# The routed experts of a gated block: order of gather and addition on GpSimd, row numbers cast on VectorE, gated rows turned inside the up products

## The reference

```python
xn = _rmsnorm(x, w_ln2)
shared = mean(_experts(xf, sWg, sWu, sWd))          # one shared expert, all rows
probs = softmax(xf @ Wgate + expert_bias)           # 8 experts
topk_p, topk_i = top_k(probs, 2)                    # two experts a row, shares scaled to sum 1
# _experts: silu(x @ Wg) * (x @ Wu) @ Wd, with 512 -> 256 -> 512
routed = einsum('ne,nec->nc', comb, _experts(xf, Wg, Wu, Wd))
x + tanh(g_ffn) * (residual + shared + routed)
```

## Time and profile before

| what | value |
|---|---|
| timed runs | 2496.61, 2498.39, 2503.72 us; median 2498.39 |
| the profiled execution's own time | 2492.11 us |
| its span, first to last instruction | 2490.3 us |
| TensorE busy | 2193.2 us (88% of the span) |
| VectorE, ScalarE, GpSimd busy | 61%, 48%, 56% |
| TensorE's granted clock, mean | 0.959 of full speed |

### The profile page before, as it was taken

One profiled execution on the slowest core, in us unless ns is written; L12 is line 12 of the kernel. 1 busy time (PEld: TensorE's weight loads), 2 busy tenths in 40 slices (PEclk: granted clock), 3 DMA queues, 4 the chain that ended last, 5 costly groups with the idle time before them and its releaser, 6 DMA issues. The chain is left out here.

```text
span 2490.3 us, 50414 instructions
## 1 busy us (share of the span) xinstructions
PE 2193.2 (88%) x12864; PEld 977.9 (39%) x12865; DVE 1506.9 (61%) x4072; ACT 1201.2 (48%) x2316; POOL 1401.2 (56%) x1598
## 2 busy tenths in 40 slices
PE   3699999999999963899999999999948887898887
PEld 1233333333333211444444444444424443444443
DVE  4588888887888733656655566565526783333332
ACT  3255555555555433354544545455445653444443
POOL 3177767677676751365654655546534664555554
PEclk9899999999999986999999999999978898999999
DMA  4413223232232204452533524334234764555554
GB/s 155 151 48 111 90 87 109 72 107 96 86 116 71 71 26 130 140 147 86 151 118 111 147 90 146 116 118 130 80 107 86 165 148 91 97 93 93 94 92 79
DMA packets 221402, 264.60 MB, mean 106 GB/s; under 512 B 37400, under 2 KB 163468, under 8 KB 220852
## 3 DMA queue, kind: packets, MB, share of 16 engines
q1 hardware_dynamic: 197628, 212.81, 28.2%
q0 software_dynamic: 22976, 48.38, 11.3%
q10 hardware_dynamic: 520, 0.27, 0.0%
HBM read 162.12 MB, written 86.80 MB: 100 GB/s over the span
## 5 line engine op out<-in xcount | busy, mean ns | idle before, releaser
L464 ACT ACTIVATE a_pt<-a_bank 128x512 f32<-128x512 f32 x512 | 305.1, 597 | 361.2 <-DVE a_bank L567 349.2
L1345 DVE CUSTOM_DVE_ANT_0 b_bank<-b_bank,b_tri 128x256 f32<-128x256 f32 (+3 forms) x512 | 253.7, 498 | 322.2 <-PE b_bank L1483 319.8
L578 DVE CUSTOM_DVE_ANT_0 a_bank<-a_bank,a_strip 128x512 f32<-128x512 f32 x512 | 354.8, 693 | 21.5 <-PE a_bank L721 18.8
L1130 POOL TENSOR_TENSOR b_acc<-b_acc,b_pt 128x256 f32<-128x256 f32 (+2 forms) x384 | 271.7, 725 | 105.6 <-ACT b_pt L1219 88.9
L374 POOL TENSOR_TENSOR a_acc<-a_acc,a_pt 128x512 f32<-128x512 f32 x256 | 317.6, 1271 | 12.8 <-ACT a_pt L464 9.3
L567 DVE TENSOR_TENSOR a_bank<-a_bank,a_band 128x256 f32<-128x256 f32 (+1 forms) x512 | 205.9, 403 | 132.3 <-PE a_bank L708 130.5
L1219 ACT ACTIVATE b_pt<-b_bank 128x256 f32<-128x256 f32 (+2 forms) x384 | 143.3, 381 | 203.5 <-PE b_bank L1467 199.5
L721 PE MATMUL a_bank<-a_k_stack,a_q_stack 97*128 97x512 f16 x512 | 197.7, 387 | 17.5 <-DMA a_k_stack<-mask_rows 10.7
L708 PE MATMUL a_bank<-a_q_stack,a_k_stack 128*128 128x512 f16 x512 | 197.6, 387 | 15.4 <-ACT a_pt L464 11.4
L1812 POOL DMA_INDIRECT out_dram<-c_z,c_to_row x72 | 115.1, 1598 | 144.1 <-DMA out_dram<-c_z,c_to_row 117.0
L2203 DVE SCALAR_TENSOR_TENSOR c_hid<-c_th,c_bank 128x256 f32<-128x256 f32 x72 | 30.3, 421 | 229.6 <-ACT c_th L1954 228.2
(11 more groups left out here) (337 smaller groups left out, 5632.7 us busy)
## 6 DMA issues: line engine op xcount, KB each, us to landing
b_q_stack<-qk_rows SPq DMA_DIRECT2D x192, 128.0 KB, 2.7
a_q_stack<-qk_rows SPq DMA_DIRECT2D x96, 128.0 KB
a_k_stack<-qk_rows SPq DMA_DIRECT2D x96, 128.0 KB
b_k_stack<-qk_rows SPq DMA_DIRECT2D x96, 128.0 KB, 2.6
a_xn<-in_x SPq DMA_DIRECT2D x32, 256.0 KB, 2.6
a_cn<-in_ctx SPq DMA_DIRECT2D x32, 256.0 KB, 3.1
qk_rows<-a_qk_hi SPq DMA_DIRECT2D x64, 128.0 KB, 1.7
qk_rows<-a_qk_lo SPq DMA_DIRECT2D x64, 128.0 KB, 1.8
```

The source lines that it names most:

```text
L464: nc.scalar.activation(pt[:, n % SLOTS, :], st_bank[n % 2][:], ACT.Exp).then_inc(exped, 1)
L578: nc.vector.tensor_tensor_reduce(out=max_bank[step % 2][:], in0=max_bank[step % 2][:], in1=strip[:, g * HG + hh, at:at + S], scale=-1.0, s ...
L1130: nc.gpsimd.tensor_tensor(sums_of, sums_of, probs(n), ALU.add).then_inc(pooled, 1)
L1345: nc.vector.tensor_tensor_reduce(out=max_bank[step % 2][:, 0:w], in0=max_bank[step % 2][:, 0:w], in1=tri[:, at:at + w], scale=-1.0, scalar ...
```

## The change

On GpSimd the gather of block j+3 stands ahead of the addition of block j-2, the casts of both kinds of row numbers are gone, and the register for the landing is loaded ahead of the waits. VectorE casts the row numbers: four `from_row` ahead of the loop, then that of block j+4 behind the low part of block j+1, and `to_row` of block j at the end of step j, which from the fourth block on waits for the addition four blocks before (the buffer's last reader). ScalarE scales the gathered rows of block j+2 ahead of the high hidden part of block j-1, and its output waits for `to_set`. On TensorE the gated rows are turned behind the first three of the twelve up products, and each register is loaded where its products begin. In the last batch of the dense part all eight `scatter` DMAs follow one another, the low part is on VectorE, `lay_starts` stands behind the first `activate`, and `add_to_output` of that batch stands behind the first three gathers.

```diff
--- before.py
+++ after.py
@@ -1766,6 +1766,9 @@
                 if b:
                     add_to_output(b - 1)
                 write_records(b)
+                if b + 1 == B:
+                    scatter(b, range(NT))
+                    continue
                 if b > 1:
                     scatter(b, (0,))
                 low_part(b, 0)
@@ -1782,22 +1785,19 @@
                     rms(b + 2)
                 if b == 1:
                     scatter(1, range(NT))
-            add_to_output(B - 1)
 
             def gather(at):
                 j, u = at.n, at.slot
-                pool.wait_ge(entered[u], at.use * 16 + 32)
+                pool.wait_ge(from_set, j + 1)
                 if not at.within(0, 3):
                     pool.wait_ge(x_turned, j + (AHEAD - 3))
                 pool.nop(nofuse=True)
-                nc.gpsimd.tensor_copy(from_row[:, u, :], entry[:, bass.ds(j, 1), 0]).then_inc(from_set, 1)
-                pool.wait_ge(from_set, j + 1)
-                pool.nop(nofuse=True)
                 pool.indirect_dma_start(x_in[:, u], None, z_all, bass.IndirectOffsetOnAxis(from_row[:, u, :], 0)).then_inc(gathered[u], 16)
 
             def scatter_add(at):
                 j, u = at.n, at.slot
-                nc.gpsimd.tensor_copy(to_row[:, u, :], entry[:, bass.ds(j, 1), 1]).then_inc(to_set, 1)
+                if not at.within(0, 0):
+                    landed_before = pool.value_load(block_i[0:1, 2, bass.ds(j, 1)], min_val=16, max_val=8 * NB)
                 pool.wait_ge(to_set, j + 1)
                 pool.nop(nofuse=True)
                 pool.wait_ge(y_ready, j + (AHEAD + 1))
@@ -1806,7 +1806,6 @@
                     pool.wait_ge(added[u % 2], at.use * 32 + u // 2 * 16)
                     pool.nop(nofuse=True)
                 if not at.within(0, 0):
-                    landed_before = pool.value_load(block_i[0:1, 2, bass.ds(j, 1)], min_val=16, max_val=8 * NB)
                     pool.wait_ge(added[(u + 1) % 2], landed_before)
                     pool.nop(nofuse=True)
                 pool.indirect_dma_start(out_rows, bass.IndirectOffsetOnAxis(to_row[:, u, :], 0), y_out[:, u], None, compute_op=ALU.add
@@ -1815,16 +1814,15 @@
             pool.wait_ge(out_stored[2], 32)
             for j in range(3):
                 gather(Count(0, j, 4))
+            add_to_output(B - 1)
             for i in range(3):
                 pool.wait_ge(out_stored[i], 16 * ((B - i + 2) // 3))
 
             def step(at):
+                if not at.within(NB - 3, NB):
+                    gather(at.back(-3))
                 if not at.within(0, 1):
                     scatter_add(at.back(2))
-                if at.within(NB - 3, NB):
-                    pool.sem_inc(from_set, 1)
-                else:
-                    gather(at.back(-3))
             over(pool, step)
             scatter_add(Count(0, NB - 1, 4))
 
@@ -1942,19 +1940,19 @@
                     x_high(0, 0)
                 if not at.within(NB - 1, NB):
                     x_high(j + 1, u + 1)
+                if not at.within(NB - 2, NB):
+                    scale_rows(at.back(-2))
                 if not at.within(0, 0):
                     act.wait_ge(x_hid_turned, j + AHEAD)
                     act.wait_ge(x_down, j + (AHEAD - 2))
                     nc.scalar.activation(hidden_rows(h_hi, u + 1), hid_bank[(u + 1) % 2][:, 0:I], ACT.Copy).then_inc(x_h_hi, 1)
-                if not at.within(NB - 2, NB):
-                    scale_rows(at.back(-2))
                 if not at.within(NB, NB):
                     act.wait_ge(x_up, j + (AHEAD + 1))
                     act.wait_ge(x_half, j + (AHEAD - 1))
                     nc.scalar.activation(hidden_rows(th, u), up_bank[u % 2][:, 0:I], ACT.Tanh, scale=0.5 / WS).then_inc(x_tanhed, 1)
                 if not at.within(0, 0):
                     act.wait_ge(x_down, j + AHEAD)
-                    act.wait_ge(from_set, j + 3)
+                    act.wait_ge(to_set, j)
                     nc.scalar.activation(y_out[:, last.slot], down_bank[(u + 1) % 2][:], ACT.Copy, scale=entry[:, bass.ds(last.n, 1), 2]
                                          ).then_inc(y_ready, 1)
             over(act, step)
@@ -2130,6 +2128,10 @@
                 v.scalar_tensor_tensor(out=hid[:, i, :], in0=hid[:, i, :], scalar=DOWN, in1=chunk_bank[2 * i + 1][:], op0=ALU.mult,
                                        op1=ALU.mult).then_inc(hidden, 1)
 
+            def low_part(i):
+                dve.wait_ge(h_hi_done, NI * (B - 1) + i + 1)
+                v.tensor_tensor(h_lo[:, i, :], hid[:, i, :], h_hi[:, i, :], ALU.subtract).then_inc(h_lo_done, 1)
+
             def finish_rows(b, t):
                 dve.wait_ge(downed, NT * b + t + 1)
                 dve.wait_ge(gated, NT * b + t + 1)
@@ -2158,15 +2160,18 @@
                 place_rows(b)
                 if b == 0:
                     find_spare()
+                activate(b, 0)
                 if not more:
                     lay_starts()
-                activate(b, 0)
+                    low_part(0)
                 if more:
                     low(b + 1, 0)
                     low(b + 1, 1)
                 if b:
                     up_weights(b)
                 activate(b, 1)
+                if not more:
+                    low_part(1)
                 if more:
                     low(b + 1, 2)
                     low(b + 1, 3)
@@ -2186,12 +2191,26 @@
                 v.tensor_tensor(xt_lo[:, u % 2, :, 0:P], turn_bank[u % 2][:].rearrange("p (k q) -> p k q", q=P), xt_hi[:, u % 2, :, 0:P],
                                 ALU.subtract).then_inc(x_lo_done, 1)
 
+            def set_from_row(at):
+                dve.wait_ge(entered[at.slot], at.use * 16 + 32)
+                v.tensor_copy(from_row[:, at.slot, :], entry[:, bass.ds(at.n, 1), 0]).then_inc(from_set, 1)
+
+            def set_to_row(at):
+                if not at.within(0, 3):
+                    dve.wait_ge(added[at.slot % 2], at.use * 32 + (at.slot // 2 * 16 - 16))
+                v.tensor_copy(to_row[:, at.slot, :], entry[:, bass.ds(at.n, 1), 1]).then_inc(to_set, 1)
+
+            for j in range(4):
+                set_from_row(Count(0, j, 4))
+
             def step(at):
                 j, u = at.n, at.slot
                 if at.within(0, 0):
                     x_low(0, 0)
                 if not at.within(NB - 1, NB):
                     x_low(j + 1, u + 1)
+                if not at.within(NB - 4, NB):
+                    set_from_row(at.back(-4))
                 if not at.within(0, 0):
                     w = (u + 1) % 2
                     dve.wait_ge(x_h_hi, j + AHEAD)
@@ -2205,6 +2224,7 @@
                     dve.wait_ge(x_half, j + (AHEAD + 1))
                     v.scalar_tensor_tensor(out=hidden_rows(hid, w), in0=hidden_rows(hid, w), scalar=DOWN, in1=up_bank[w][:, I:2 * I],
                                            op0=ALU.mult, op1=ALU.mult).then_inc(x_hidden, 1)
+                    set_to_row(at)
             over(dve, step)
 
         @block.tensor
@@ -2309,8 +2329,8 @@
                     last = nc.tensor.transpose(turn_bank[u % 2][:, k * P:(k + 1) * P], rows[:, k * P:(k + 1) * P], idn[:])
                 last.then_inc(x_turned, 1)
 
-            def x_up_to(j, u, e):
-                w = u % 2
+            def x_up_to(at, e):
+                j, u, w = at.n, at.slot, at.slot % 2
                 pe.wait_ge(x_lo_done, j + (AHEAD + 1))
                 pe.wait_ge(x_hidden, j + (AHEAD - 1))
                 for k in range(NK):
@@ -2319,6 +2339,8 @@
                     mm(up_bank[w][:], xt_hi[:, w, k, 0:P], weights(gu_hi), start=(k == 0), stop=False)
                     mm(up_bank[w][:], xt_hi[:, w, k, 0:P], weights(gu_lo), start=False, stop=False)
                     last = mm(up_bank[w][:], xt_lo[:, w, k, 0:P], weights(gu_hi), start=False, stop=(k == NK - 1))
+                    if k == 0 and not at.within(0, 0):
+                        turn_hidden(at.back(1).n, u + 1)
                 last.then_inc(x_up, 1)
 
             def turn_hidden(j, u):
@@ -2351,22 +2373,19 @@
 
             def step(at):
                 j, u = at.n, at.slot
-                own = earlier_x = None
                 if not at.within(NB, NB):
                     own = expert_of(at)
-                if not at.within(0, 0):
-                    earlier_x = expert_of(at.back(1))
                 if at.within(0, 0):
                     x_turn(x_in[:, 0], 0, 0)
                 if not at.within(NB - 1, NB):
                     after = at.back(-1)
                     x_turn(x_in[:, after.slot], after.n, after.slot)
+                if at.within(NB, NB):
+                    turn_hidden(at.back(1).n, u + 1)
+                else:
+                    x_up_to(at, own)
                 if not at.within(0, 0):
-                    turn_hidden(at.back(1).n, u + 1)
-                if not at.within(NB, NB):
-                    x_up_to(j, u, own)
```

(3 more changed lines are left out.)

## The result

The changed kernel takes 2433.9 us (median of 4, 2432.3 to 2436.6) against 2497.5 for the kernel before on the same chip: ratio 0.9743 (95%: 0.9725 to 0.976). The forecast was 2435, with a range of 2424 to 2470. The profiled execution took 2433.8 us (span 2432.0), 58.3 under that of before.

The account below looks back on a forecast made before the run. GpSimd's own list of work was taken as the bound; 69 steps from 5.58 to 4.65 us gain 64.2, end costs 1, hand-over 0: -63 us, median 2498.4 to 2435, range 2424 to 2470.

Parts of the forecast that it names:

- The bound: Routed part: GpSimd's own list of work sets the 5.58 us per block; the landing falls beside it by chance.
- GpSimd's new turn: GpSimd's steady rhythm: between 3.20 us (lower bound, 0.30 between indirect DMAs) and 5.16 us (upper), no longer the bound.
- Rival (1): GpSimd stays the bound, its sequencer taking the pieces in series: rhythm 5.16, 2468 us; chance 0.13.
- The gather: Steady rhythm: gather issued earlier leaves 3 us in hand, so ScalarE's 2.77 us idle goes.
- TensorE's step: Routed part: floor 4.54 us plus 0.11 (0.1 ScalarE's order, 0.01 register loads) gives 4.65 per block.
- ScalarE's tight order: ScalarE and VectorE work ahead of the down products, 3.0 to 3.3 us against 3.25 available; charged 0.1 us a step.
- rival (5): TensorE isn't freed, its register loads or loop turns showing under thin cover: rhythm 5.2 to 5.3, 2475 us; chance 0.04.
- The turn of the gated rows: TensorE: placed after the first quarter of up products, it has 1.0 us to spare, so the 0.52 idle goes.
- Rival (2): VectorE's new casts and GpSimd's descriptor writing hold each other up: rhythm 4.95, 2454 us; chance 0.08.
- The cover of 1.8 us: Output buffers and early gather absorb blocks waiting for landings, 0.9 us over rhythm twice running; cost nothing, 14 us otherwise.
- End: Last output scaling to last addition: additions lag a little more; cost 1 us, between -1 and +4.
- Hand-over: Last dense batch to first routed blocks: first gather gains 2 to 3 us, fourth loses it; sum 0, -3 to +4.

Follow-up runs that it names:

- e2_casts_on_gpsimd: The changed kernel with both casts of row numbers back on GpSimd, each right ahead of its DMA: 2470.0 us, ratio 0.9877.
- e1_addition_first: The changed kernel with the addition ahead of the gather on GpSimd again, casts still on VectorE: 2507.5 us, ratio 1.0019.
- e10_scaling_last: The changed kernel with ScalarE's old order, the high hidden part ahead of the scaling of gathered rows: 2429.6 us, ratio 0.9712.
- e5_registers_front: The changed kernel with both of TensorE's register loads at the front of the step again: 2480.0 us, ratio 0.9923.
- e8_own_behind_turn: The changed kernel with TensorE's first register load put behind the turn of the next block's rows: 2437.1 us, ratio 0.9751.
- e3_turn_ahead: The changed kernel with the gated rows turned ahead of all up products again: 2442.4 us, ratio 0.976.
- c0_changed_again: The same changed program, nothing edited, in a second profiled execution: span 2425.9 us.

## Why the prediction was right, step by step

**The bound.** Right. Before the change the additions trailed their output scalings by 3.3 to 4.2 us in 55 of 71 turns and by 2.8 or more in 67, so outputs lay ready; a register load moved on GpSimd alone gave 24.6 us; and the list's turn after is 3.18 us, where the lower bound was 3.20. The chain of waits in the earlier trace rows was a coincidence, as the prediction took it.

**GpSimd's new turn.** Right, at the lower bound: 0.30 ahead of the gather for the 0.79 of the earlier trace rows. The Trainium skill ("Perfetto Trace Analysis", DMA Instruction — SWDGE (GPSIMD)) has the sequencer free for the next instruction once the DMA is pushed; the trace agrees, by this 0.30. Rival (1), 2468, is nearly what `e2_casts_on_gpsimd` gave (2470).

**The gather.** Right: ScalarE waits 0.9 us in total for gathered rows in the routed part, where it waited 180. The time in hand was what decided. It was 3 us by the prediction, with a landing of 3.65; the gathers now land 4.3 us after their start in the median, and ScalarE takes them up at 6.6, so 2.3 were in hand. It ran out once: one gather landed only after 5.9 us and reached ScalarE 0.69 late, and TensorE's step there is the one of 5.55. The prediction weighed this order by its own and didn't say that, with ScalarE's new order and the old one on GpSimd, the loop closes over two blocks; `e1_addition_first` shows 70 us for it.

**TensorE's step.** The sum was right: 4.65 forecast, 4.66 measured between additions and 4.63 between TensorE's own first turns. Its two terms were right in size as well, but not in how they act. ScalarE's tight order was charged 0.1 a step and costs 5.3 us over 66 steps, 0.08 (`e10_scaling_last`); what is left there at the loop's turn is 0.6 us, the 0.01 of the register loads. But an ordinary step loses nothing to ScalarE's order: the down products wait for their low part twice in the part, 1.5 us in total. It is lost at the loop's turn, 4.95 and then 4.59 where 4.54 would stand twice. From the low part's end to the start of the down products it is 1.6 us in the kernel before (median), 0.34 in the changed kernel and 0.61 in `e10_scaling_last`; TensorE's sequencer waits for that low part, and only 1.3 us of down products are queued when it comes to branch and register load. It is the mechanism of rival (5), at 6 us for its 40.

What the prediction had wrong is what moving the second register load was worth. It took both to be hidden behind queued matmuls and charged 0.01; in the changed kernel both loads at the front cost 0.68 us a step, 47 us in all (`e5_registers_front`). That didn't touch the forecast, as the load was moved in the change, and so far the hit is luck. That the low part's lateness is what uncovers the loads rests on `e5_registers_front`, `e8_own_behind_turn` and `e10_scaling_last`; both loads at the front under ScalarE's old order weren't tried, nor the kernel before with one load moved.

**The turn of the gated rows.** The idle 0.52 went, as forecast, but it goes without that edit too (`e3_turn_ahead`, 4.69). That it had come of ScalarE's late scaling, as rows 4 read, fits this and wasn't tested by itself.

**VectorE.** Rival (2) fell. From the sixth low part on the trace has 127 of the new casts; 90 start beside an indirect DMA of GpSimd, and all take 0.14 to 0.15 us. Here is one of the first in the timeline of the changed kernel:

```profile
2079.84 0.14 DVE L2196 CAST c_from_row<-c_entry 128x1 int32<-128x1 f32 x1
```

The Trainium skill's exclusive lock ("SBUF — State Buffer", Who interferes with whom) shows in no row of this change. The output scaling now waits for the `to_row` cast 46 times, 48.3 us in all, which I had not priced. The additions still come 1.6 to 1.8 us after it and TensorE isn't kept waiting, so it costs nothing visible; no run takes this wait out.

**Landings.** The cover of 1.8 us held: 20 intervals of 5.34 us or more, made up for by 8 of 3.18 and by short ones. TensorE's mean step is 4.63 through them all, and the steps over 4.6 stand at the loop's turn but for one of 4.65.

**The ends.** End: last output scaling to last addition 5.2 us for 5.65, so a gain of 0.5 where 1 was charged. Hand-over: from the first records of the last batch to the first addition 44.75 before, 46.68 after (47.19 in `c0_changed_again`), so +1.9 within -3 to +4. TensorE's first turn comes 3.2 us earlier in it and the fourth gather gives it back, as the prediction says. That gather reaches ScalarE at 2089.4, and with the dense part 5.6 us late in this execution the forecast of 2083 stands for 2088.6. The steady part was multiplied by 69 steps, where 71 intervals gained: 65.7 for 64.2.

## What to carry to other kernels

When a chain of waits names a landing, set the waiting instruction beside the engine's own list and beside the work that it could have waited for; one of them keeps a constant distance. Price a register load or a loop's turn by what is queued ahead of it after the sequencer's last wait, not by whether it is hidden today: 47 us here. What the parts of a change are worth doesn't add up: undone singly, three of them cost 70, 47 and 34 us of a gain of 63.

## What the runs showed of the hardware

A gather takes longer to land when it is issued right behind an addition: 4.3 us from its start (median by the view of DMAs) in the changed kernel, where 0.30 us lie between the addition's end and the gather, and 3.7 in `e2_casts_on_gpsimd`, where it is 1.00. To ScalarE's use it is 4.39 in the row of `e1_addition_first` and 3.65 in the kernel before. Why is open. Two indirect DMAs with a register load between them still follow by 0.30 us, so that load costs nothing there; behind a cast of the same engine the gap is 0.79 to 0.80. And the first records of the last dense batch, with nothing ahead of them that the change touches, came at 2042.3 to 2056.0 us in the profiles of these kernels; between two executions of the same changed program they differed by 6 us, and between four profiles on one chip by as much. So a pair of profiles can't settle a term of 5 us, while a stretch counted from a common instruction can.
